# Two graph layers on one core: values moved to the tile's end, three buffers for h, a mask in two parts, and x and adjacency loads issued after the spread of target scores

## What is computed

```python
# layer 0: 12 heads of 64
h = einsum('bnd,ade->bane', x, W);  th = tanh(h)
attn = (th @ w_src) + swap(th @ w_dst)            # one score per pair of nodes and head
attn = softmax(where(~adj, -999, leaky_relu(attn, 0.2)))
feat = elu(attn @ h + b)
gate = sigmoid(x @ H_w.T + H_b)
x = layernorm(x + gate * feat + (1 - gate) * x)
# layer 1: 6 heads of 128, q, k, v, masked softmax, output product, residual, layernorm
```

## Time and profile before

| what | value |
|---|---|
| runs, median of 3 | 2741.1 us (2740.21 to 2742.04) |
| profiled execution, its own time | 2743.32 us |
| profiled execution, span of the instructions | 2741.6 us |
| PE busy, share of the span | 99% |
| DVE, ACT, POOL busy | 61%, 44%, 34% |
| granted TensorE clock | 0.999 of full |

### The profile page before, as it was taken

The page is one execution under the profiler, slowest core; times in us unless marked ns, Lnnn a source line. Parts: engine busy times, 40 slices in busy tenths (PEclk is TensorE's granted clock), DMA queues, the critical chain, the costliest instruction groups (busy, mean ns, idle before and its releaser), DMA issues.

```text
span 2741.6 us, 51890 instructions
## 1 busy us (share of the span) xinstructions
PE 2720.1 (99%) x20988; PEld 2513.6 (92%) x20988; DVE 1676.8 (61%) x3335; ACT 1211.7 (44%) x3109; POOL 926.6 (34%) x566
## 2 busy tenths in 40 slices
PE   8999999999999999999999999999999999999998
PEld 7777778878888899999999999999999999999998
DVE  7899998888888764444444444444544444444443
ACT  5666676666666743233332333233332333233332
POOL 2353334434444223323332333323332333323330
PEclk9999999999999999999999999999999999999999
DMA  6655665555555522222222222222232222222220
GB/s 186 171 137 145 164 158 143 140 140 140 137 141 139 189 65 67 73 82 71 59 82 70 72 69 67 73 82 71 59 82 71 80 61 68 73 82 71 59 70 24
DMA packets 306896, 269.50 MB, mean 98 GB/s; under 512 B 227809, under 2 KB 244193, under 8 KB 306657
## 3 DMA queue, kind: packets, MB, share of 16 engines
q1 hardware_dynamic: 306656, 266.19, 35.5%
HBM read 142.65 MB, written 75.89 MB: 80 GB/s over the span
## 4 chain that ended last, share of the span: by engine, by line
PE 88%; DVE 5%; DMA 3%; issue 2%; ACT 2%; SPq 1%; POOL 0%; DVEq 0%; ACTq 0%; POOLq 0%
PE ps_hg L1069 21%; PE ps_k L70 15%; PE ps_a L70 15%; PE ps_q L70 15%; PE ps_a L1244 15%; PE ps_s L1185 2%; PE ps_c L1210 2%; PE ps_pv L1101 1%; DMA dst_all<-dst_scratch 1%; ACT logits L567 1%; PE ps_t L1088 1%; PE ps_pt L1210 1%; DMA dst_scratch<-dst 1%; PE ps_pt L1192 1%; DVE logits L792 1%
## 5 line engine op out<-in xcount | busy, mean ns | idle before, releaser
L1069 PE MATMUL ps_hg<-w_hi,xT 128*128 128x512 f32 x2268 | 745.6, 401 | 4.5 <-DVE h_one L825 4.2
L1069 PEld LDWEIGHTS ps_hg<-w_hi,xT 128*128 128x128 f32 x2268 | 426.2, 188 | 108.1 <-issue 6.7
L1069 PE MATMUL ps_hg<-w_lo,xT 128*128 128x512 f32 x1134 | 448.4, 395 | 0.0
L70 PE MATMUL ps_k<-x1T_hi,wk_hi 128*128 128x256 f32 x1152 | 329.0, 286 | 0.0
L70 PE MATMUL ps_k<-x1T_lo,wk_hi 128*128 128x256 f32 x1152 | 321.8, 279 | 0.0
L70 PE MATMUL ps_k<-x1T_hi,wk_lo 128*128 128x256 f32 x1152 | 321.1, 279 | 0.0
L70 PE MATMUL ps_q<-x1T_hi,wq_hi 128*128 128x256 f32 x1140 | 319.3, 280 | 0.0
L70 PE MATMUL ps_q<-x1T_lo,wq_hi 128*128 128x256 f32 x1140 | 318.5, 279 | 0.0
L70 PE MATMUL ps_q<-x1T_hi,wq_lo 128*128 128x256 f32 x1140 | 317.8, 279 | 0.0
L497 POOL TENSOR_TENSOR th_src<-th,wsrc_all 128x768 f32<-128x768 f32 x64 | 118.3, 1849 | 479.9 <-DVE dst_all L805 462.1
L657 ACT ACTIVATE qT<-ps_q,bq_col 128x256 f32<-128x256 f32 x192 | 80.5, 470 | 451.6 <-PE ps_q L70 451.6
(11 more groups left out here) (156 smaller groups left out, 5747.3 us busy)
## 6 DMA issues: line engine op xcount, KB each, us to landing
x_tok<-x SPq DMA_DIRECT2D x64, 384.0 KB, 4.1
dst_all<-dst_scratch SPq DMA_DIRECT2D x128, 192.0 KB, 3.4
gate_scratch<-gate SPq DMA_DIRECT2D x64, 384.0 KB, 2.6
feat_scratch<-feat SPq DMA_DIRECT2D x128, 192.0 KB, 2.8
feat_in<-feat_scratch SPq DMA_DIRECT2D x62, 384.0 KB, 3.1
gate_in<-gate_scratch SPq DMA_DIRECT2D x62, 384.0 KB, 3.7
x_even<-x SPq DMA_DIRECT2D x16, 768.0 KB, 4.2
x_odd<-x SPq DMA_DIRECT2D x16, 768.0 KB, 4.4
```

Of the source, the lines that this page charges most:

```text
L70: ins = pe.matmul(out, left[a][c], right[b][c], start=(n == 0), stop=(n == len(terms) - 1))
L1069: ins = pe.matmul(ps_hg[:, cols], left[a][c], right[b][c], start=(c == 0 and n == 0), stop=(c == KC - 1 and n == 2))
```

## The change

- PE: `values(T - 2)` moves behind `project(2)`, directly ahead of `transpose_probs(T - 1)`; the semaphore increments stay with their instructions.
- DVE: `attention`, `elu`, and ACT's `elu_exp`, run for tile T - 3 instead of T - 2, from T = 3 on. The tail: `attention(61)` ahead of `softmax_scores(63)`, `elu(61)` behind it, `elu_exp(61)` behind `copy_probs(62)` on ACT; `elu(60)` in the last tile of the loop.
- `h_one` has three places (tile modulo 3); the memory comes from `th_src`, which goes: POOL multiplies in place in `th`. ACT's tanh waits for `src_done` instead of `thsrc_done`.
- DVE: mask and maximum in two parts, the four heads of DVE ahead of the wait for ACT's eight, the eight behind it: two instructions more in each tile.
- SP: `spread_dst(T)` directly behind `turn_x(T + 2)`; `load_x(T + 3)` and `load_adj(T + 2)` behind it; `store_feat` one tile later.

```diff
 # SP, loop over T
                 if TURNED <= T + 2 < NT:
                     turn_x(T + 2)
-                    if T + 3 < NT:
-                        load_x(T + 3)
+                spread_dst(T)
+                if TURNED <= T + 2 and T + 3 < NT:
+                    load_x(T + 3)
                 if T + 2 < NT:
                     sp.wait_ge(mask_done, T + 1)
                     load_adj(T + 2)
-                spread_dst(T)
...
-                if 2 <= T < NT - 1:
-                    store_feat(T - 2)
+                if 3 <= T < NT - 1:
+                    store_feat(T - 3)
...
 # SP, after the loop
             sp.wait_ge(z_done, NT)
+            sp.wait_ge(pv_done, NT - 2)
             feat_and_gate(1, 0)
...
+            store_feat(NT - 4)
             store_feat(NT - 3)
 # POOL
-                if T >= 1:
-                    pool.wait_ge(src_done, T)
-                pool.tensor_tensor(th_src[:, :], th[:, :], wsrc_all[:, :], ALU.mult).then_inc(thsrc_done, 1)
+                pool.tensor_tensor(th[:, :], th[:, :], wsrc_all[:, :], ALU.mult).then_inc(thsrc_done, 1)
 # ACT
                     act.wait_ge(thdst_done, T)
-                    act.wait_ge(thsrc_done, T)
+                    act.wait_ge(src_done, T)
...
                 exp_scores(T - 1)
-                if T >= 2:
-                    elu_exp(T - 2)
+                if T >= 3:
+                    elu_exp(T - 3)
...
             copy_probs(NT - 2)
+            elu_exp(NT - 3)
             act.wait_ge(cols_in, 48)
 # DVE
+            def masked_max(T, part, first, last):
+                n = last - first
+                scores_ = per_head(logits[:, first * NODES:last * NODES], n)
+                dve.copy_predicated(
+                    scores_, not_adj[:, T % 2, :].unsqueeze(1).to_broadcast([P, n, NODES]),
+                    masked[:, 0:1].unsqueeze(2).to_broadcast([P, n, NODES])).then_inc(masked_done, 1)
+                dve.wait_ge(masked_done, 2 * T + part + 1)
+                dve.tensor_reduce(neg_max[:, first:last], scores_, AX_X, ALU.max, negate=True).then_inc(max_done, 1)
...
-                dve.wait_ge(prelu_done, T + 1)
                 dve.wait_ge(leaky_done, T + 1)
                 dve.wait_ge(mask_done, T + 1)
...
+                masked_max(T, 0, ON_ACT, HEADS0)
+                dve.wait_ge(prelu_done, T + 1)
+                masked_max(T, 1, 0, ON_ACT)
+                dve.wait_ge(max_done, 2 * (T + 1))
...
-                if T >= 2:
-                    dve.wait_ge(pv_done, T - 1)
-                dve.tensor_tensor(h_one[:, T % 2, :, 0:E0], per_head(ps_hg[:, 0:D], HEADS0),
+                if T >= 3:
+                    dve.wait_ge(pv_done, T - 2)
+                dve.tensor_tensor(h_one[T % 3][:, :, 0:E0], per_head(ps_hg[:, 0:D], HEADS0),
...
-                if T >= 2:
-                    attention(T - 2)
+                if T >= 3:
+                    attention(T - 3)
                 if T > 2:
                     bias_h(T)
                 if T == NT - 1:
                     bias_g(T)
+                    elu(T - 3)
                     break
...
+            attention(NT - 3)
+            softmax_scores(NT - 1)
             elu(NT - 3)
-            softmax_scores(NT - 1)
             attention(NT - 2)
 # PE, loop over T
                 project(1, T).then_inc(h_done, 1)
+                project(2, T).then_inc(g_done, 1)
                 if T >= 2:
                     values(T - 2)
-                project(2, T).then_inc(g_done, 1)
                 if T >= 2:
                     transpose_probs(T - 1)
```

More of the change, by code:

```diff
@@ L151, in two_graph_layers @@
         th = at(S + 21504, "th", [P, D])
[L152 to L155, removed]
+        h_hole = at(S + 24576, "h_hole", [P, HEADS0, EW])
+        Hb_less1 = at(S + 27712, "Hb_less1", [P, D])
+        dst_all = at(S + 30784, "dst_all", [P, D])
         th_dst = dst_all
-        logits = at(S + 33792, "logits", [P, D])
+        logits = at(S + 33856, "logits", [P, D])
         probs = logits
[L159 to L171, removed]
+        h_one = [at(S + 36928, "h_one0", [P, HEADS0, EW]), h_hole, at(S + 40064, "h_one2", [P, HEADS0, EW])]
+        probsT = at(S + 43200, "probsT", [P, HEADS0, NODES])
+        att = at(S + 46272, "att", [P, D])
+        ones = at(S + 46272, "ones", [P, P])
+        feat = at(S + 49344, "feat", [P, D])
+        gate = at(S + 52416, "gate", [P, D])
+        adj_u8 = at(S + 55488, "adj_u8", [P, 4, NODES], U8)
+        not_adj = at(S + 55744, "not_adj", [P, 2, NODES], U8)
+        dst = at(S + 55872, "dst", [P, HEADS0])
+        src = at(S + 55936, "src", [P, 2, HEADS0])
+        neg_max = at(S + 56032, "neg_max", [P, HEADS0])
+        row_inv = at(S + 56096, "row_inv", [P, 2, HB])
+        masked = at(S + 56160, "masked", [P, 1])
+        b_less1 = at(S + 56192, "b_less1", [P, E0])
         x1T_hi = at(S, "x1T_hi", [P, KC, GN], F32R)
@@ L588, in mask_of @@
                 if T >= 2:
-                    act.wait_ge(masked_done, T - 1)
+                    act.wait_ge(masked_done, 2 * (T - 1))
                 act.activation(not_adj[:, T % 2, :], adj_u8[:, T % 4, :], ACT.Copy, scale=-1.0, bias=1.0).then_inc(mask_done, 1)
@@ L830, in src_scores @@
                 dve.wait_ge(thsrc_done, T + 1)
-                dve.tensor_reduce(src[:, T % 2, :], per_head(th_src[:, :], HEADS0), AX_X, ALU.add).then_inc(src_done, 1)
+                dve.tensor_reduce(src[:, T % 2, :], per_head(th[:, :], HEADS0), AX_X, ALU.add).then_inc(src_done, 1)
             def bias_g(T):
@@ L890, in _ @@
             dve.memset(masked[:, :], MASKED0).then_inc(fixed, 1)
-            dve.memset(h_one[:, :, :, E0:EW], 1.0).then_inc(fixed, 1)
+            for place in h_one:
+                dve.memset(place[:, :, E0:EW], 1.0).then_inc(fixed, 1)
             rest_x(0)
@@ L895, in _ @@
             dve.wait_ge(memsets, 2)
-            dve.wait_ge(fixed, 2)
+            dve.wait_ge(fixed, 4)
             bias_h(0)
@@ L919, in _ @@
                 bias_g(T)
-                if T >= 2:
-                    elu(T - 2)
+                if T >= 3:
+                    elu(T - 3)
                 for t in range(GT):
@@ L1101, in values @@
                             ins = pe.matmul(ps_pv[graph(half), g, k * EW:(k + 1) * EW], probsT[graph(g), a, :],
-                                            h_one[graph(g), T % 2, a, :], start=True, stop=True)
+                                            h_one[T % 3][graph(g), a, :], start=True, stop=True)
                 ins.then_inc(pv_done, 1)
```

## The result

The changed kernel takes 2755.5 us (2754.78 to 2757.7, five runs) against 2741.1 before: a ratio of 1.0054, 95% interval 1.0043 to 1.0066. It is 14.4 us slower, and the prediction had 2737.0 with a range up to 2743.0. The profiled execution took 2755.49 us for a span of 2753.7.

A forecast was written before the change was run, and what follows sets the result against it. PE, busy 99% of the span, was taken as the bound. PE edit -2.5, stalls -2.5 and hand-over +0.85 summed to -4.1, so 2741.1 became 2737.0 us; the 8-in-10 range was 2730.5 to 2743.

The forecast's parts named there:

- The PE edit: PE in steady stage 0: values directly ahead of transposes give a 14.27 us tile, gain 0.04, 2.5 us over 62 tiles.
- 0.86 over the 1.03: PE, values to transposes: 0.86 us taken, since the trace's 1.03 was held to be a wait for ACT's exponential.
- the 0.63: PE, transposes to the next matmul when directly behind values: 0.63 us, taken instead of 0.57.
- the drain rule: PE: changing tiling mode drains TensorE; the edit keeps two changes a tile, so by this rule alone gains 0.
- The hand-over: From stage 0 to stage 1: exponential and transposes of tile 63 come 0.85 us later, ends 0 and 1.5.
- Stage 1 isn't touched: The stage behind the hand-over: no change expected there; a change would make the prediction wrong in kind.
- The new wait for att: PE's values at tile's end against DVE's attention: 4.18 against 4.20 us, a tie, taken as 0 in steady tiles.
- the stalls of the other tiles: PE's waits in stage 0, 5.94 us before: expected gain 2.5 us, ends 0 and 5.
- Rival 4: Stage 0: the new wait for att decides, at 0.3 us a tile, giving 2755.6 us; chance 0.10.
- (a): DVE's mask in two parts: reaches tanh's end some 0.5 us earlier, worth nothing in steady tiles, 0.5 in late ones.
- (b): SP's x load no longer ahead of the store of target scores: `dst_in` 0.7 us earlier, ends 0 to 0.8.
- (c): POOL's join earlier, x split later: DVE's low part of x alone, 0.5 us less; split lands on mask and maximum.

The follow-up runs named there:

- e10: e2 with values(T - 2) back between project(1) and project(2): 2742.1 us, ratio 1.0000.
- e11: The same kernel as e2, run again on another chip: 2738.9 us, ratio 0.9989.
- e1: The changed kernel with the store of feat of tile 60 issued on SP ahead of the feat and gate reads and six Wv chunks: 2746.4 us.
- e7: The changed kernel with 72 unused matmuls filling PE's gap between values of tile 62 and transposes of tile 63: 2753.4 us, ratio 1.0041.
- e2: e1 with attention(T - 3) moved to the start of tile T on VectorE, ahead of rest_x(T + 1): 2738.3 us, ratio 0.9988.
- e3: e1 with mask and maximum in one part again: 2747.5 us.
- e6: The kernel before the change with only mask and maximum in two parts: 2742.3 us, ratio 1.0000.
- e9: e2 with mask and maximum in one part: 2737.9 us, ratio 0.9988.
- e8: e2 with SP's old order, loads of x and adjacency ahead of the spread of target scores: 2747.3 us, ratio 1.0014.

## Why the prediction was wrong

**The PE edit: right.** Forecast 0.04 us a tile and 2.5 in all, measured 0.05 and 3.1 (e10 against e11). The choice of 0.86 over the 1.03 of the earlier trace rows, as a wait for the exponential, holds, and so does the 0.63. By the drain rule of the Trainium skill (TensorEngine Tiling (Array Packing), Key Properties) this would have been 0. The number of tiling changes is the same and the time is not, so the rule alone doesn't price a change of neighbours; what it says of the drain isn't contradicted.

**The hand-over: the step that failed, and the largest.** The prediction put `elu_exp(61)` "inside its wait of 1.29 and a little more" and costed it at its 1.7 us of work; 0.85 us late in all. It did not follow that instruction's own wait, `feat_stored`. In the loop this wait is free, because the store was issued a tile earlier. At the hand-over the change writes the store behind six weight loads, and the wait became 8.8 us. e1 shows 9.1 us for it by the medians and 11.3 by the traces, of which the drop of the clock is 2.8 (e7); that drop is a term that the forecast did not have. "Stage 1 isn't touched" failed with it: its first query matmuls ran at the granted clock of 0.50. The forecast's work on ACT was about right: in e1, where the store comes in time, PE waits 0.6.

**The new wait for att: the tie was seen, its price was not.** The forecast took 0 in steady tiles, and they show 14.262. But it let the stalls of the other tiles fall from 5.9 to 3.4 (0.9 in tile 3 or 4, 1.7 with the mixing, 0.8 with the weight chunks), and they rose to 9.2 (1.9, 3.7, 3.2 and 0.4 behind them). This is the second step that failed: PE waits 7.8 us for att in 13 places, where 2 to 4 us in tiles 3 and 12 to 16 were forecast, and the largest part of what was missed, 2.4 us, stands in the tiles with weight chunks. Moving the attention ahead takes 8.1 us off (e2), 5.8 of stalls in the traces. Rival 4 named this wait and 2755.6 us, and the time hit that number, but by chance: it wanted 0.3 us in every tile, and a steady tile loses nothing.

**What gives VectorE air, (a) to (c).** (b) was right in its row: the store to spread fell (74.4 us of waits instead of 120.1), 0.71 a tile:

```profile
SPq L329 <- DMA dst_scratch<-dst: 74.4, 64, 1.9
```

(c) was right that the low part of x runs alone at 0.96, and wrong that this is air: VectorE then waits that much longer for ACT, while the split's new place costs 0.7 us a tile in the addition and the leaky step together. The forecast had the split on the mask and the maximum; both kept their time beside it (four-head mask 0.51 to 0.52 us in 25 tiles beside the split, 0.50 to 0.52 in the 39 others). (a) gives nothing measurable (e3, e6, e9).

**The sum.** By the traces of the profiled executions: pace -3.1, the other stalls of stage 0 -1.7 (4.2 in e2 instead of 5.9), ACT's and VectorE's work at the hand-over +0.5, attention's place +5.0 (9.2 instead of 4.2), store and clock +11.3: 12.0, for the 12.1 us by which the span grew. By the medians: -3.1, 9.1 and 8.1, 14.1 for 14.4. This second sum closes because e10, which has all of the change but the place of the values, with the two edits of e2, takes the time of before (2742.1 and 2741.9); so the medians don't confirm the 1.7. The three places for h and POOL's product in place have no run of their own.

## What to carry to other kernels

When a step is moved later by one round of a loop, follow every wait that the step itself carries, and above all in the hand-written tail, where the producer may stand behind bulk transfers in a queue. When a PE instruction moves, its old place may have been hiding how late its inputs are: compare the slack in every kind of tile, not in the steady one. And two edits that each shift a transfer and its reader have to be tried together, since e2's gain is lost when SP's old order comes back (e8). A forecast can also hit a number by another way: the shown waits, and not the total, tell which term was right.

## What was not expected of the hardware

The order of neighbours on PE has a price of its own: six transposes take 0.57 us behind a projection and 0.63 behind the values, and yet the whole tile is 0.05 shorter, since the second projection matmul no longer comes 0.34 after the first. A single stand of 9.2 us cost 2.8 us more through the granted clock, which was 0.50 from within the gap until 6 us after work had begun again, at 952.52. And POOL's copies cost VectorE time in some operations and none in others: means of 881 ns instead of 426 in the leaky step and 1972 instead of 948 in elu, both with all operands in SBUF (the 15 leaky steps beside no POOL instruction took 0.42 to 0.43 us, the longest that overlapped the split 1.74), while the sums by head and the gate's bias, which reads PSUM, kept their 0.95 beside the join.
